# Edge products of a graph attention layer in one fp32r pass over four stacked terms, with a group sum moved ahead of a product on TensorE

## The reference, cut to what matters

```python
w_m = (efeat @ W_msg + b_msg).reshape(E, 16, 16)     # E = 103125 edges, efeat has 16 features
w_a = (efeat @ W_attn + b_attn).reshape(E, 16, 16)
h_src = feat[src][:, :, None]                        # the source node's 16 features
e1, e2 = w_m * h_src, w_a * h_src
ex = exp(e2 - segment_max(e2, dst)[dst])
attn = ex / segment_sum(ex, dst)[dst]
ft = segment_sum(e1 * attn, dst).sum(axis=1)         # summed over the 16 input features
```

## Time and profile before

| | |
|---|---|
| three executions | 2708.16, 2709.70, 2709.81 us; median 2709.7 us |
| profiled execution | span 2774.5 us from its first to its last instruction; the page gives no other time of it |
| busy share of the span | VectorE 81%, TensorE 79%, ScalarE 64%, GpSimd 48% |
| `layer1_sum` | from 729 to 971 us of the span |
| attention | from 1090 to 2710 us of the span, its 44 blocks |

### The profile page before, as it was taken

The page is one execution under the profiler, slowest core; times in us unless marked ns, Lnnn a source line. Parts: engine busy times, 40 slices in busy tenths (PEclk is TensorE's granted clock), DMA queues, the critical chain, the costliest instruction groups (busy, mean ns, idle before and its releaser), DMA issues. The chain is left out here.

```text
span 2774.5 us, 36642 instructions
## 1 busy us (share of the span) xinstructions
PE 2191.1 (79%) x7895; PEld 960.2 (35%) x7896; DVE 2233.7 (81%) x3857; ACT 1763.9 (64%) x6869; POOL 1321.9 (48%) x1141
## 2 busy tenths in 40 slices
PE   1688888898699984488888888888888888888870
PEld 0344444466455532123222222222222222222220
DVE  7799999314587702399999999999999999999996
ACT  6577777013111111588888888888888888888843
POOL 5000000405550002577767777677777777777704
PEclk9899999888899996588888888888888888888885
DMA  3000000205785431012222222222222222222214
GB/s 69 6 0 0 0 0 0 93 1 177 244 259 179 139 116 23 19 52 71 71 71 71 71 71 71 70 63 71 71 71 71 71 71 71 71 71 71 66 57 123
DMA packets 109221, 205.35 MB, mean 74 GB/s; under 512 B 38652, under 2 KB 66980, under 8 KB 103406
## 3 DMA queue, kind: packets, MB, share of 16 engines
q1 hardware_dynamic: 67278, 156.49, 16.0%
q0 software_dynamic: 41888, 48.19, 8.0%
HBM read 76.22 MB, written 128.34 MB: 74 GB/s over the span
## 5 line engine op out<-in xcount | busy, mean ns | idle before, releaser
L1803 POOL DMA_INDIRECT hs<-h_table,gix x860 | 1081.6, 1258 | 434.5 <-issue 241.8
L1914 ACT ACTIVATE e<-wps,hs 128x32 f32<-128x32 f32 x5632 | 1030.6, 404 | 227.5 <-PE wps L1844 158.9
L1844 PE MATMUL wps<-w_edge,ef 18*128 18x512 f32 x1760 | 578.8, 706 | 301.1 <-ACT e L1914 162.6
L1866 PE MATMUL slot_sums<-e,ident 128*128 128x512 f32 x1392 | 757.0, 694 | 8.5 <-DVE e L2018 7.0
L1866 PEld LDWEIGHTS slot_sums<-e,ident 128*128 128x128 f32 x1392 | 294.8, 223 | 489.0 <-issue 463.7
L1844 PEld LDWEIGHTS wps<-w_edge,ef 18*128 18x128 f32 x1760 | 159.3, 200 | 678.1 <-ACT e L1914 309.8
L526 ACT CAST edges<-acc 128x400 f32 x600 | 295.0, 492 | 102.0 <-PE acc L513 75.3
L509 PE MATMUL acc<-q_hot,lo_hot 128*128 128x400 bf16 x1200 | 307.4, 338 | 53.3 <-DVE q_hot L483 51.4
L1953 DVE TENSOR_TENSOR e<-wps,hs 128x2048 f32<-128x2048 f32 x132 | 301.6, 2285 | 54.9 <-remote 23.0
L551 POOL DMA_INDIRECT got<-in_edge_rows,start x64 | 65.1, 1018 | 543.9 <-POOLq L464 417.6
L483 DVE TENSOR_SCALAR q_hot<-qcol,qT 128x400 bf16<-128x400 bf16 x1200 | 290.5, 317 | 1.0 <-PE acc L513 0.9
(11 more groups left out here) (381 smaller groups left out, 1964.0 us busy)
## 6 DMA issues: line engine op xcount, KB each, us to landing
rows_state<-states SPq DMA_DIRECT2D x43, 1280.0 KB
rows_shift<-shifts SPq DMA_DIRECT2D x44, 640.0 KB
got_order<-edges_order SPq DMA_DIRECT2D x56, 256.0 KB
ef_order<-efT SPq DMA_DIRECT2D x56, 256.0 KB
hs<-h_table,gix POOLq DMA_INDIRECT x880
ef<-ef_order SPq DMA_DIRECT2D x44, 320.0 KB
edges_order<-got POOLq DMA_DIRECT2D x32, 256.0 KB
edges_order<-msg_parts POOLq DMA_DIRECT2D x24, 256.0 KB
```

The source lines that it names most:

```text
L1803: nc.gpsimd.indirect_dma_start(out=hs[u][:, s, :], out_offset=None, in_=d["h_table"], in_offset=bass.IndirectOffsetOnAxis(ap=gix[u][:, s:s ...
L1844: nc.tensor.matmul(wps[:, bank, :], ef[u][k:k + KM, g * P:(g + 1) * P], w[k:k + KM, :], start=True, stop=True).then_inc(a_mult, 1)
L1866: ins = nc.tensor.matmul(sums[:, g % 2, :], ident[:, :], e[u][:, g * SLOTS + c, :], start=(c == 0), stop=(c == SLOTS - 1))
L1914: ins = nc.scalar.mul(e[u][:, s, at], wps[:, bank, at], hs[u][:, s, f:f + 1])
```

## The change

The features and the weights of the edge products are each split into a high part, rounded to fp32r, and the remainder. Four terms (high x high, low x high, high x low, low x low) are stacked along the contraction: 72 rows instead of 18, all from partition 0, and one fp32r matmul instead of an fp32 one. `layer1_sum` makes both parts: ScalarE's copy writes the rounded part, VectorE subtracts it from `tr`, and SP stores both; one buffer each instead of two. `attention_edges` loads each part twice, in four DMAs for a block, and makes the stacked weights once. On TensorE the sum of a block's group 1 moves from the head of a period to the end of the period before, ahead of the product of slot 15. (Semaphore declarations are only moved in `prepare_pairs`.)

```diff
-            "ef_order": dram("ef_order", [SLOTS * KE, GORDER, P], F32),
+            "ef_high": dram("ef_high", [SLOTS * KE, GORDER, P], F32),
+            "ef_low": dram("ef_low", [SLOTS * KE, GORDER, P], F32),
...
-        efT = [sb(f"efT{v}", [SLOTS * KE, TURN, P]) for v in range(2)]
+        high, low = (sb(n, [SLOTS * KE, TURN, P], F32R) for n in ("efT_high", "efT_low"))
...
-                        sp.dma_start(d["ef_order"][:, groups, :], efT[r % 2][:, :, :]).then_inc(u_stored[r % 2], 16)
+                        sp.dma_start(d["ef_high"][:, groups, :], high[:, :, :].bitcast(F32)
+                                     ).then_inc(u_stored, 16)
+                        sp.wait_ge(y_low, turn + 1)
+                        sp.dma_start(d["ef_low"][:, groups, :], low[:, :, :].bitcast(F32)
+                                     ).then_inc(u_low_stored, 16)
...
-                                    pe.wait_ge(y_evac, j * TURNS_IN_CHUNK + r)
+                                    pe.wait_ge(y_low, j * TURNS_IN_CHUNK + r)
...
-                        if r >= 2 or later:
-                            act.wait_ge(u_stored[r % 2], (j * 2 + r // 2) * 16)
-                        nc.scalar.copy(efT[r % 2][:, :, :], tr[:, :, :]).then_inc(y_evac, 1)
+                        if r or later:
+                            act.wait_ge(u_stored, j * (TURNS_IN_CHUNK * 16) + r * 16)
+                        nc.scalar.copy(high[:, :, :], tr[:, :, :]).then_inc(y_evac, 1)
...
                         turn = j * TURNS_IN_CHUNK + r
+                        if turn:
+                            remainder(turn - 1)
...
+                def remainder(turn):
+
+                    dve.wait_ge(y_evac, turn + 1)
+                    if turn:
+                        dve.wait_ge(u_low_stored, turn * 16)
+                    nc.vector.tensor_tensor(low[:, :, :], tr[:, :, :], high[:, :, :].bitcast(F32), ALU.subtract
+                                            ).then_inc(y_low, 1)
...
-        w = sb("w_edge", [P, 2 * CH])
+        TERMS = ("high", "low", "high", "low")
+        KS = len(TERMS) * KM
+        w_in = sb("w_edge", [KM, 2 * CH])
+        w_high, w_low = sb("w_high", [KM, 2 * CH], F32R), sb("w_low", [KM, 2 * CH], F32R)
+        w = sb("w_terms", [KS, 2 * CH], F32R)
...
-        ef = [sb(f"ef{u}", [P, BG * P]) for u in range(2)]
+        ef = [sb(f"ef{u}", [KS, SLOTS, BG * P], F32R) for u in range(2)]
...
-                    sp.dma_start(ef[u][:, :], ef_t[:, cols(b, BG * P)]).then_inc(a_ef[u], 16)
+                    for n, term in enumerate(TERMS):
+                        sp.dma_start(ef[u][n * KM:(n + 1) * KM, :, :].bitcast(F32),
+                                     ef_t[term][0:KM, :, cols(b, BG * P)]).then_inc(a_ef[u], 16)
...
+                sp.wait_ge(a_split, 2)
+                for n, part in enumerate((w_high, w_high, w_low, w_low)):
+                    sp.dma_start(w[n * KM:(n + 1) * KM, :].bitcast(F32), part[:, :].bitcast(F32)).then_inc(a_terms, 16)
...
-                    g, k = s // SLOTS, s % SLOTS * KE
-                    nc.tensor.matmul(wps[:, bank, :], ef[u][k:k + KM, g * P:(g + 1) * P],
-                                     w[k:k + KM, :], start=True, stop=True).then_inc(a_mult, 1)
+                    g, c = s // SLOTS, s % SLOTS
+                    nc.tensor.matmul(wps[:, bank, :], ef[u][:, c, g * P:(g + 1) * P], w[:, :],
+                                     start=True, stop=True).then_inc(a_mult, 1)
...
-                def period(u, b, before):
+                def period(u, b, before, following):
...
-                    add(1)
                     for_act(u, b, (4,))
                     add(0)
...
-                    for_act(u, b, (13, 14, 15))
...
+                    for_act(u, b, (13, 14))
+                    if following is not None:
+                        summed(1 - u, following, 1)
+                    for_act(u, b, (15,))
...
-                        period(u, i * 2 + (2 + u), i * 2 + u)
+                        period(u, i * 2 + (2 + u), i * 2 + u, i * 2 + (u + 1))
...
+                dve.wait_ge(a_w, 16)
+                nc.vector.tensor_copy(w_high[:, :], w_in[:, :]).then_inc(a_split, 1)
+                dve.wait_ge(a_split, 1)
+                nc.vector.tensor_tensor(w_low[:, :], w_in[:, :], w_high[:, :].bitcast(F32), ALU.subtract
+                                        ).then_inc(a_split, 1)
```

More of the change, by code:

```diff
@@ L16 @@
 F32 = mybir.dt.float32
+F32R = mybir.dt.float32r
 BF16 = mybir.dt.bfloat16
@@ L250, in prepare_pairs @@
         tr = prep.enter_context(nc.psum_tensor("tr", [P, PAIR_TILES, 4, P], F32))
+        b_rows = [sem("b_rows0"), sem("b_rows1")]
+        b_gather = sem("b_gather")
         b_consts, b_cast, b_blank, b_ends, b_node = (sem("b_" + n) for n in "consts cast blank ends node".split())
-        b_loaded, b_x, b_pairs, b_gather, b_stripdma = (sem("b_" + n) for n in "loaded x pairs gather stripdma".split())
+        b_loaded, b_x, b_pairs, b_stripdma = (sem("b_" + n) for n in "loaded x pairs stripdma".split())
         b_dve, b_pe, b_last, b_coarse, b_groups = (sem("b_" + n) for n in "dve pe last coarse groups".split())
         b_fine, b_rank, b_after, b_nought = sem("b_fine"), sem("b_rank"), sem("b_after"), sem("b_nought")
-        b_rows = [sem("b_rows0"), sem("b_rows1")]
         with nc.Block() as block:
@@ L1204, in layer1_sum @@
         u_load = [sem("u_load0"), sem("u_load1")]
-        u_stored = [sem("u_stored0"), sem("u_stored1")]
-        y_turned, y_evac, y_copied, y_masked, y_moved = (sem("u_" + n) for n in "turned evac copied masked moved".split())
+        u_stored, u_low_stored = sem("u_stored"), sem("u_low_stored")
+        y_turned, y_evac, y_low, y_copied, y_masked, y_moved = (
+            sem("u_" + n) for n in "turned evac low copied masked moved".split())
         lent = parts[:, 1, :, :, :].rearrange("p t a n -> p (t a n)")
@@ L1266, in _ @@
                 sp.wait_ge(m_store, 16 * 2 * CHUNKS)
-                for s in u_stored:
-                    sp.wait_ge(s, 16 * CHUNKS * TURNS_IN_CHUNK)
+                for stored in (u_stored, u_low_stored):
+                    sp.wait_ge(stored, 16 * 2 * CHUNKS * TURNS_IN_CHUNK)
             @block.gpsimd
@@ L1367, in _ @@
                     chunk(j)
+                remainder(2 * CHUNKS * TURNS_IN_CHUNK - 1)
                 v = Line(dve, m_dve)
@@ L1715, in attention_edges @@
             sem("a_" + s) for s in "w mult read_v read_s sub exp weighed sum halved acc shift last step go".split())
-        a_marks, a_x = sem("a_marks"), sem("a_x")
+        a_marks, a_x, a_terms, a_split = sem("a_marks"), sem("a_x"), sem("a_terms"), sem("a_split")
         a_gix = [sem("a_gix0"), sem("a_gix1")]
@@ L1725, in attention_edges @@
         GM = 16 * BLK
+        EF = 16 * len(TERMS)
         shifts_t = d["rows_shift"].rearrange("(p j) c -> p j c", p=P)
         states_t = d["rows_state"][0:GTOTAL, :].rearrange("(p j) c -> p j c", p=P)
-        ef_t = d["ef_order"].rearrange("k g p -> k (g p)")
+        ef_t = {n: d["ef_" + n].rearrange("(c k) g p -> k c (g p)", c=SLOTS) for n in ("high", "low")}
         src_t = src[:, :, :].rearrange("p g c -> p (g c)")
@@ L1749, in _ @@
                 sp.dma_start(marks[:, :, :].rearrange("p g m -> p (g m)"), d["marks"]).then_inc(a_marks, 16)
-                for c in range(SLOTS):
-                    sp.dma_start(w[c * KE:c * KE + KM, :], io["w_edge"]).then_inc(a_w, 16)
+                sp.dma_start(w_in[:, :], io["w_edge"]).then_inc(a_w, 16)
                 def features(u, b):
-                    sp.dma_start(ef[u][:, :], ef_t[:, cols(b, BG * P)]).then_inc(a_ef[u], 16)
+                    for n, term in enumerate(TERMS):
+                        sp.dma_start(ef[u][n * KM:(n + 1) * KM, :, :].bitcast(F32),
+                                     ef_t[term][0:KM, :, cols(b, BG * P)]).then_inc(a_ef[u], 16)
                 def store_shifts(u, b):
@@ L1888, in period @@
                     for_dve(u, b, 2, NV + 2)
-                    for_act(u, b, (13, 14, 15))
[L1891 to L1895, removed]
+                    for_act(u, b, (13, 14))
+                    if following is not None:
+                        summed(1 - u, following, 1)
+                    for_act(u, b, (15,))
+                pe.wait_ge(a_terms, 16 * len(TERMS))
+                pe.wait_ge(a_ef[0], EF)
+                period(0, 0, None, None)
+                pe.wait_ge(a_ef[1], EF)
+                period(1, 1, None, 0)
                 with pe.Fori(0, BLOCKS // 2 - 1) as i:
                     for u in range(2):
-                        pe.wait_ge(a_ef[u], i * 16 + 32)
-                        period(u, i * 2 + (2 + u), i * 2 + u)
-                for g in (1, 0, *range(2, BYPE)):
+                        pe.wait_ge(a_ef[u], i * EF + 2 * EF)
+                        period(u, i * 2 + (2 + u), i * 2 + u, i * 2 + (u + 1))
+                for g in (0, *range(2, BYPE)):
                     summed(0, BLOCKS - 2, g)
```

## The result

The changed kernel takes 2885.71 us in the median (2883.73 to 2887.72) against 2708.93 us for the kernel before beside it: a ratio of 1.0646, interval 1.0633 to 1.0658. It is slower, as forecast, by 177 us and not by 111; the time lies 16 us above the range. The profiled execution has a span of 2882.0 us. One thing is needed to read this: the profiled execution of before that the prediction went by (span 2774.5 us) was about 65 us longer than the timed ones, and a second profile of the same kernel, shown with the experiments, was not.

What follows compares the result with a forecast made beforehand. VectorE, 94% busy, was taken to bound the attention, with slot 15 on its path. Attention +101 (42 blocks x 2.4), `layer1_sum` +8 and start +2 gave +111 on 2774.5, scaled to 2819 us; range 2750 to 2870.

Steps and rivals of the forecast that it cites:

- The chain: Attention, group 1 weighed to second `largest`: hand-over, moved sum 6.1, product 15 0.6, slot 15 2.95, hand-overs; 9.85 us against 6.5.
- What would show it: Attention marks: period near 37.6 us, L1973 wait 3 or more, L2053 near nothing, sum 5 to 7 at 0.50, VectorE under 0.90.
- The block before: Attention block of the kernel before: 35.19 us, with 6.5 from weighing to second `largest` and 0.96 wait before `accumulate` 0.
- `layer1_sum`: Stage before the attention: added VectorE subtraction overfills the second half, first half fits; +8 us, bounds 0 and +28.
- The start: Attention's start: weights pass through SBUF, first product some 3 us later, ScalarE 2 us late; +2 us, bounds 0 and +6.
- A block's loads: Attention: four DMAs and 737 KB a block instead of one and 320 KB, needed a period later; costs nothing.
- The price of an fp32r pass: Attention products: one pass between 0.23 and 0.43 us for 512 columns; VectorE's four 1.2 to 2.0 in sequence, costed at nothing.
- The clock is up when the sum starts: Rival, attention: moved sum 3.65 us, chain 7.3, -0.2 a block; 2701 us, or 2712 with +10 ahead; chance 0.16.
- break-even of 4.3 us: Clock rival, attention: it decides where moved sum and product 15 together stay under 4.3 us.
- The dear pass: Rival, attention: an fp32r pass costs a record or more, product 15 at 1.2; +1.0 a block, +42, 2861 us; chance 0.08.
- The transfers of `layer1_sum`: Rival: 256 KB more a turn has no room in the first half; 26 us in place of 8, 2837 us; chance 0.06.

Runs made afterwards that it cites:

- the store going first: Changed kernel with the old sum order, and SP issuing the high store of a `layer1_sum` turn before the next load: 2705.80 us, ratio 0.9982 to before.
- products alone: Changed kernel with group 1's sum back at the head of a period, fp32r products kept: 2718.07 us, ratio 1.0025 to before.
- The fill: Changed kernel plus 24 useless matmuls a block into an idle bank, between group 3's sum and the moved one: 2797.53 us, ratio 1.0318 to before.
- order alone: Kernel before with only group 1's sum moved ahead of product 15, fp32 products kept: 2857.51 us, ratio 1.0531 to before.
- one more VectorE step: Changed kernel plus a VectorE `memset` of about 0.5 us a block behind `rescale`: 2886.56 us, ratio 1.0648 to before.

## Why the prediction was right and where it was wrong

**The chain: right.** It was to take 9.85 us; measured are 10.07. The sum starts 0.13 us after the weighing and takes 6.69, above the 6.1 and below the bound of 7 (the first profile's sums are 5.84 in the mean and not 5.7, which changes little); slot 15 begins 7.09 after the weighing, 0.27 behind the sum's end. All five marks of "What would show it" came: block 37.52 against 37.6, the wait 3.93 against "3 us or more", the other at 0.00, the sum right at the weighing and at 0.50, VectorE at 0.88. That the block came out within 0.1 us says less than it seems: with half a microsecond more of VectorE work it was 37.53 too, so here a plain sum of steps is not what sets it.

**The block before: the step that failed.** "A block takes 1442.87 / 41 = 35.19 us" was true of one execution, and so were the 6.5 us and the 0.96 from which +2.4 a block follows. By the second profile the chain is 6.06 and the wait 0.46; a block gets 3.38 us longer, and 41 x 3.38 = 139 us stand in place of 101: 38 of the 67 us between 2819 and 2885.71. The prediction saw that the span stood 65 us above the median, but carried the sum over as if those 65 us lay outside the blocks or scaled with them. They lay, for 43 us, in the very waits that the change removes or covers: the changed kernel's block was predicted well, and the kernel before had less to lose.

**`layer1_sum`: the other step that failed, its first half.** The term was +8, bounds 0 to 28; the stage grew by 26.7 (269.1 against 242.4), 19 us more than forecast. The windows of the second profile of before and of after, each from the stage's first cast to its 27th and from there to its last, columns as in the earlier trace rows, show where:

```profile
740.80:855.00 114.20, 106.27 (x593) 60.13 (x592) 85.27 (x209) 18.45 (x33) 53.51 (x64) 0.98 0.81 255
855.00:972.40 117.40, 117.40 (x662) 67.40 (x661) 93.94 (x235) 20.74 (x37) 0.00 (x0) 0.98 0.46 142
```

```profile
737.70:871.50 133.80, 111.28 (x596) 60.04 (x595) 103.33 (x238) 17.84 (x33) 52.88 (x64) 0.96 0.82 268
871.50:996.30 124.80, 118.61 (x659) 65.36 (x658) 109.90 (x258) 20.10 (x37) 0.00 (x0) 0.99 0.59 193
```

The second half grew by 7.4 us, near the +8, but by luck: the +8 came from a VectorE that is full there, and it is busy in 109.90 of 124.80 us, while the store going first took back 5.5 of the 8.6 us by which this half grew in products alone (117.4 to 126.0). The first half, while GpSimd still fetches, grew by 19.6, and there the prediction put nothing: "In the first half it fits (86.29 + 18), unless the extra 256 KB a turn slow the loads". Two things came to it. One is the single buffer, costed at nothing as well. The cast waits for the store of the turn just before, whose issue stands behind a load: 4.23 us a turn in the ring shown above, from the second half, against 4.0. That this costs time is shown by the store going first. The other is the transfers: 268 GB/s x 133.8 us is 35.9 MB, against 29.1 before, and at the 255 GB/s of before the 6.8 MB more are 26 us, an estimate. No run separates the two, so what holds the 17.6 us that are left of 28.5 with the store first stays open; VectorE's subtraction, which TensorE's next transpose into `tr` waits for, may have a part in it, and that is argued only.

**Smaller terms.** The start was +2 and is +3.0 (from the stage's end to block 1's second `largest`, 205.3 against 202.3 us). The tail adds 3.9. With an earlier start of `layer1_sum` of 2.9 us the account closes for the two profiled executions: 138.6 + 26.7 + 3.0 + 3.9 - 2.9 = 169.3 = 2882.0 - 2712.7. The other 7.5 of the 177 are these executions' distances from their medians. A block's loads are 720 KB in the page's KB, not 737; nothing hangs on it.

**The price of an fp32r pass: right at the lower bound.** VectorE's four take 1.20 us in a row, where the old four side by side took 1.14; three steps of 0.23 and a last record of 0.50 make that. So the products cost nothing, as forecast. The Trainium skill ("FP8 and Floating Point Precision", TensorE Precision Notes) counts four passes for fp32. The trace agrees with about a quarter: 0.23 us for one fp32r product against two fp32 records of 0.43 by the prediction's reading.

**The rivals.** "The clock is up when the sum starts" is out: of the 43 moved sums the first takes 5.56 us, the next two 6.20 and 6.45 and all others 6.58 to 6.75, and the one shown ran at 0.50 but for its last 0.61 us. That "all sums but the first of a block run at 1.00", which spoke for this rival, was not quite so: in the first profile the fourth took 5.2 to 5.3 us, against 3.70, in more than a quarter of the blocks. This rival wouldn't have saved the sign either. Its break-even of 4.3 us came from the first profile; by the second, sum and product 15 would have to fit into 6.06 + 0.46 - 2.95 - 0.20 = 3.4 us, and a sum at full clock takes 3.60 by itself. The fill shows it: with sums of 3.69 us the block is still 0.40 us longer than before. The dear pass is out by the 0.23. The transfers of `layer1_sum` are not out: the first half's +19.6 us lie near the 26 that this rival put there, and the order of two issues, though it moved 10.9 us in all, brought back only about half of that in the first half.

## What to carry to other kernels

Before you put work ahead of a product, ask who waits for that product: TensorE's order is a queue, and 6.7 us of sum ahead of 0.3 us of product went straight onto VectorE's path, though the sum itself was wanted early. Check the profiled execution against the timed ones, and when it is longer, find in which waits the excess lies before you carry a sum over from it. And a buffer cut from two to one closes a ring of write, issue queue, transfer and landing; add that ring up, and compare it with a turn, in each stretch of the stage: the transfers beside it can differ.

## What was not expected of the hardware

Three kernels whose steps differ have the same block: 37.52 us with fp32r products, 37.55 with fp32 ones (from the moved sum's end to slot 15 1.09 us, against 0.27), 37.53 with half a microsecond more VectorE work. Each time the moved sum took up the difference (6.69, 5.90, 6.23 us). The granted clock is at 0.50 when the sum starts in each and rises before the sum ends in each. The windows of the moved sum up to the rise and from there to its end: the changed kernel in the block behind the one above, then order alone, then one more VectorE step:

```profile
1979.70:1985.80 6.10, 6.10 (x7) 2.52 (x8) 5.98 (x6) 2.67 (x16) 3.80 (x2) 0.50 0.05 4
1985.80:1986.41 0.61, 0.61 (x3) 0.35 (x2) 0.00 (x0) 0.00 (x0) 0.00 (x0) 1.00 0.00 0
```

```profile
1955.60:1960.05 4.45, 4.45 (x6) 1.85 (x7) 4.45 (x5) 2.66 (x15) 3.80 (x2) 0.50 0.05 4
1960.05:1961.49 1.44, 1.44 (x6) 0.44 (x4) 1.41 (x2) 0.00 (x0) 0.00 (x0) 1.00 0.05 6
```

```profile
1946.58:1951.72 5.14, 5.14 (x6) 2.19 (x7) 5.11 (x6) 2.67 (x16) 3.79 (x2) 0.50 0.04 5
1951.72:1952.81 1.09, 1.09 (x4) 0.54 (x3) 0.87 (x1) 0.00 (x0) 0.00 (x0) 1.00 0.00 0
```

In the changed kernel the clock rises at 1948.25 in one moved sum and at 1985.80 in the next, 37.55 us later, and that is the length of the block. The same distance from moved sum to moved sum comes out of the other two traces (1960.05 to 1997.60, 1951.72 to 1989.26). The changed kernel comes to it step by step: behind block 1 its blocks take 37.07, 37.29, 37.41, 37.48 and 37.51 us, then 37.55, and their moved sums 6.20, 6.45, 6.58, 6.64 and 6.68, then 6.71; what is missing halves about from block to block. That fits rises whose distance the kernel's steps don't set: a sum that starts x later does less at half clock before the rise, work worth x/2 at full clock, and so ends x/2 later. So work put ahead of the rise was given back behind it, and the block kept the length of the rises. This is read from the rows and not tested further, and what sets the distance is open.

The landing of one and the same 256 KB store went from 2.3 us, first in its turn on SP, to 3.2 behind a load and 3.6 from ScalarE's queue.
